# Mamba scan with a mixture of experts, one core: the load order and one pair of adds inside the scan's tile loop

## The reference

```
x = x + mamba2(layernorm(x)) + moe(layernorm(x))
```

```
Y_diag = einsum(C, B, L, xdt)          # inside a block of tokens, L the decays between two tokens
states = einsum(B, decay_states, xdt)  # what the block adds to the state
carry  = carry * chunk_decay + states  # from block to block
Y_off  = einsum(C, prev_carry, exp(dA_cs))
y = (Y_diag + Y_off + x * D) * silu(z);  y = rmsnorm(y) * norm_w;  out = y @ out_proj.T
```

## Time and profile before

| what | us |
|---|---|
| median of 3 runs | 727.1 (726.68 to 730.82) |
| the profiled execution, its own time | 727.78 |
| its span, first to last instruction | 726.0 |
| PE busy in the span | 644.9 (89%) |
| DVE busy | 509.1 (70%) |
| ACT busy | 373.9 (51%) |
| POOL busy | 316.3 (44%) |

### The profile page before, as it was taken

The page is one execution under the profiler, slowest core; times in us unless marked ns, Lnnn a source line. Parts: engine busy times, 40 slices in busy tenths (PEclk is TensorE's granted clock), DMA queues, the critical chain, the costliest instruction groups (busy, mean ns, idle before and its releaser), DMA issues.

```text
span 726.0 us, 12653 instructions
## 1 busy us (share of the span) xinstructions
PE 644.9 (89%) x4189; PEld 530.0 (73%) x4190; DVE 509.1 (70%) x1116; ACT 373.9 (51%) x787; POOL 316.3 (44%) x223
## 2 busy tenths in 40 slices
PE   4867899999999999999999999888478999999992
PEld 3757769778786777867977877564347889889981
DVE  4965976887887697788798798878866644434430
ACT  3653973754656467276375463647035644444441
POOL 1110144544452553525454425255363565665642
PEclk9968999999999999999999999999778999999996
DMA  8940112230430420403223203093277667676663
GB/s 253 332 142 29 58 61 79 97 117 30 145 118 22 154 107 12 145 32 116 99 78 117 100 18 117 1 273 105 76 207 206 113 121 141 116 132 128 116 101 43
DMA packets 32051, 80.91 MB, mean 111 GB/s; under 512 B 4801, under 2 KB 10049, under 8 KB 29825
## 3 DMA queue, kind: packets, MB, share of 16 engines
q1 hardware_dynamic: 22176, 55.22, 23.2%
q0 software_dynamic: 9056, 21.50, 16.4%
q10 hardware_dynamic: 768, 3.54, 1.6%
HBM read 60.45 MB, written 19.79 MB: 111 GB/s over the span
## 4 chain that ended last, share of the span: by engine, by line
PE 54%; DVE 13%; issue 11%; DMA 8%; ACT 6%; POOL 5%; SPq 1%; DVEq 0%; POOLq 0%; ACTq 0%
PE pi L1415 15%; PE pg L1605 11%; PE po L1454 8%; PE pd L1618 7%; DMA e<-cs_d 7%; DVE xs L917 3%; PE px L1588 2%; PE py L1492 2%; PE py L1499 2%; ACT m L647 2%; PE pxb L1572 2%; POOL y L511 1%; POOL ysq L478 1%; DVE y L1197 1%; PE phs L1628 1%
## 5 line engine op out<-in xcount | busy, mean ns | idle before, releaser
L1415 PE MATMUL pi<-xh,whl 128*128 128x256 f32 x1152 | 169.6, 291 | 5.3 <-DVE zs L923 2.8
L1415 PEld LDWEIGHTS pi<-xh,whl 128*128 128x128 f32 x1152 | 150.6, 194 | 8.6 <-issue 5.4
L917 DVE SCALAR_TENSOR_TENSOR xs<-raw,conv_w,xs 128x256 f32<-128x256 f32 x240 | 110.3, 525 | 14.3 <-ACT xs L622 14.3
L1454 PE MATMUL po<-wo,y 128*128 128x512 f32 x256 | 114.7, 601 | 2.2 <-DVE cbm L1220 1.5
L1415 PE MATMUL pi<-xl,whl 128*128 128x256 f32 x576 | 93.3, 285 | 0.0
L1454 PEld LDWEIGHTS po<-wo,y 128*128 128x128 f32 x256 | 48.1, 193 | 57.2 <-issue 55.3
L531 POOL DMA_INDIRECT out<-yo,idx x39 | 63.0, 1617 | 55.6 <-ACT yo L777 29.8
L1415 PEld LDWEIGHTS pi<-xl,whl 128*128 128x128 f32 x576 | 80.1, 192 | 0.0
L647 ACT ACTIVATE m<-m,cs_tok 128x128 f32<-128x128 f32 x256 | 79.6, 388 | 0.5
L1605 PE MATMUL pg<-ew,xgh 128*128 x312 | 66.1, 355 | 0.0
L506 POOL TENSOR_TENSOR carry<-carry,cd 128x1024 f32<-128x1024 f32 x15 | 29.0, 1934 | 84.2 <-PE py L1492 84.1
(11 more groups left out here) (203 smaller groups left out, 1180.0 us busy)
## 6 DMA issues: line engine op xcount, KB each, us to landing
m<-cs_d SPq DMA_DIRECT2D x16, 1024.0 KB, 5.6
e<-cs_d SPq DMA_DIRECT2D x32, 256.0 KB, 4.9
w_as_read<-in_w_in SPq DMA_DIRECT2D x9, 512.0 KB, 8.2
res<-in_x SPq DMA_DIRECT2D x16, 256.0 KB, 2.8
out<-o SPq DMA_DIRECT2D x16, 256.0 KB
ew<-in_w_gu SPq DMA_DIRECT2D x5, 768.0 KB, 8.9
xin<-in_x SPq DMA_DIRECT2D x6, 512.0 KB, 3.7
xn_d<-xin SPq DMA_DIRECT2D x6, 512.0 KB, 2.8
```

Of the source, the lines that this page charges most:

```text
L917: dve.scalar_tensor_tensor(out=xs[par][:, b, :], in0=raw[:, b, k:k + GT], scalar=conv_w[:, b, k:k + 1], in1=xs[par][:, b, :], op0=ALU.mult ...
L1415: mm = pe.matmul(bank[:, hf, :], whl[:, weight(g, n), lo, k, hf * P:(hf + 1) * P], xx[:, k, :], start=k3 == 0, stop=k3 == 11)
L1454: mm = pe.matmul(po[:, :], y[:, b, :], wo[:, b, :], start=b == 0, stop=b == XB - 1)
```

## The change

It does two things. In SP's loop `load_decays2(t)`, the two loads of e2 for tile t, stands ahead of `load_x(g + 2)` and of `load_decays(t + 1)`, the next tile's m; before it stood behind both. And the wait for `cdec` and `st` with the two adds to the carried state are a function `carried`, which DVE calls in even tiles ahead of `finish(t - 1)` and `own(1)`, and in odd tiles where it stood, behind `own(1)`.

```diff
                 if t == 0:
                     load_decays(1)
+                if t:
+                    load_decays2(t)
                 if c == 0 and g + 2 < G:
                     load_x(g + 2)
                 if 0 < t < T - 1:
                     load_decays(t + 1)
-                if t:
-                    load_decays2(t)
                 if c == 0 and g + 2 < G:
                     store_xn(g + 2)
...
+                def carried():
+                    dve.wait_ge(cdec, t + 1)
+                    dve.wait_ge(st, t + 1)
+                    for half in range(2):
+                        sl = carry[:, 4 * half:4 * half + 4, :, :].rearrange("p b a d -> p (b a d)")
+                        dve.tensor_tensor(sl, pxb[half][:, :, :].rearrange("p b l -> p (b l)"), sl,
+                                          ALU.add).then_inc(cadd, 1)
...
                 for n in taken[2:3]:
                     stage(g + 1, n)
+                if c == 0:
+                    carried()
                 if t:
                     finish(t - 1)
...
                 own(1)
                 if t == T - 1:
                     break
-                dve.wait_ge(cdec, t + 1)
-                dve.wait_ge(st, t + 1)
-                for half in range(2):
...
+                if c == 1:
+                    carried()
```

More of the change, by code:

```diff
@@ L1291, in vector @@
                     break
-                dve.wait_ge(cdec, t + 1)
-                dve.wait_ge(st, t + 1)
-                for half in range(2):
-                    sl = carry[:, 4 * half:4 * half + 4, :, :].rearrange("p b a d -> p (b a d)")
-                    dve.tensor_tensor(sl, pxb[half][:, :, :].rearrange("p b l -> p (b l)"), sl,
-                                      ALU.add).then_inc(cadd, 1)
+                if c == 1:
+                    carried()
                 for n in taken[3:4]:
```

## The result

The changed kernel has a median of 751.1 us over 4 runs (744.41 to 753.49), the kernel before on the same chip 726.9 (726.17 to 730.82). The ratio is 1.0307 with a 95% interval of 1.0230 to 1.0384: slower, by more than the predicted range held. The profiled execution took 749.91, its span is 748.1 against 726.0, its mean granted clock 0.955 against 0.962.

A forecast was written before the change was run, and what follows sets the result against it. PE was taken to bound the scan. The terms -2.9 + 4.0 + 0.9 + 0.5 = +2.5 us gave 730.3 for the profiled execution, and 729.6 as the predicted median, range 721.5 to 737.

The forecast's parts named there:

- the load of m in the odd tiles: m, issued behind buffer e2 in odd tiles, is 0.9 us late for DVE; hidden up to tile 11, cost nothing.
- the even tiles: Earlier load of buffer e2 returns tiles 6 and 8 to 26.75 us, load_x issued as before: -2.9 us.
- tile 13: No router there and PE already stops at off(1), so m's 0.9 us lateness goes through: +0.9 us.
- The adds' price of 4.0: Odd tiles 3 to 11: early adds push own(1), POOL's add and buffer e2, so PE waits at join: +4.0 us.
- Only PE's stops are to be had: Whole scan: it is bound by PE at a granted clock of 1.00, so only its stops can be gained.
- so the stop of 1.0 goes: Start of odd tiles: adds end at 266.6, before PE's transposes at 267.25, so PE's 1.0 us wait vanishes.
- Join's own price: PE's join L1386 in odd tiles: an idle time of 1.5 to 2 us, ended by ACT L599, replaces the adds' stop.
- +0.9 and +0.5: Later m: +0.9 us in tile 13, and +0.5 us for tile 15's m, issued behind buffer e2 in tile 14.
- The third rival: m's load bounds odd tiles at L940 if landing takes over 6.8 us; 8.5 us over tiles 3 to 11, 741.3 us; chance 0.13.
- The adds' stop at tile 15 goes as well: Tile 15: the adds' stop vanishes, but DVE then waits for ACT's btok, so the effect is 0.
- The rule on the ring: DMA queue: by in-order descriptors, removing m ahead of buffer e2 would help; the trace was read as showing no earlier landing.
- The estimate of 3.2 us for e2: Buffer e2's 512 KB load: 2.0 us plus bytes at 436 GB/s gives 3.2 us; the trace's 4.0 was used.

The follow-up runs named there:

- e5: Kernel before, loads unchanged; in even tiles DVE does own(1), then the adds, then finish(t - 1): 750.5 us, ratio 1.0270.
- e3: Kernel before with the loads of buffer e2 ahead of x and m in even tiles only, adds as before: 731.7 us, ratio 1.0020.
- e2: As a run, not the buffer: kernel before with the adds alone moved as in the change, loads as before: 738.6 us, ratio 1.0120.
- e6: The adds-only kernel with L932 of the odd tile's first stage moved behind xdt: 740.1 us, measured once.
- e4: Changed kernel, but in odd tiles m is loaded ahead of buffer e2 as before: 741.6 us, ratio 1.0197 against the kernel before.
- e9: Kernel with own(1), adds, then finish in even tiles, plus m of the tile after next issued at ydiag ahead of the store: 728.4 us, ratio 1.0001.
- e10: Kernel with adds between own(1) and finish and m issued early, plus load order x, buffer e2, m in even tiles: 726.2 us, ratio 0.9975.
- e8: Kernel before, but in odd tiles the load of m also waits for yadd, so is issued right ahead of buffer e2: 748.2 us, ratio 1.0284.

## Why the prediction was wrong

The sum was +2.5 us, and the span grew by 22.1. Three terms of it failed: the load of m in the odd tiles, put at nothing up to tile 11 (7.9 us); the even tiles, put at -2.9 (+3.4); and tile 13, put at +0.9 (+5.4). The adds' price of 4.0 held in the steady tiles and failed in tile 3. A lower granted clock was in no term at all.

*"Only PE's stops are to be had", "so the stop of 1.0 goes".* The second is right: L1520 waits for nothing. The first holds in the tiles 3 to 11 of the changed kernel, where the clock stays at 1.00. It doesn't in the tiles 12 and 13 and behind 15, where 6.4 of the 7.1 us of longer busy time lie, nor in the odd tiles of e5. The prediction had the clock at 1.00 from the profile before, and put at nothing, without a word, that longer stops could lower it.

*"So that load_x is issued at 239.6 as before": -2.9.* The issue is as late as was said, 1.1 us behind e2's (243.45, then 244.58 in tile 6). But the step took the issue for the landing. Behind e2's 512 KB, x landed in 5.0 us in the median for 3.7, in e3 in 6.4, and its reader L817 waited. The even tiles lost instead: their sum is 1.6 us shorter, but it held the five stops at L1514 of 1.0 that are gone, so the rest is 3.4 us longer, 1.5 of it PE's busy time in tile 12 at the lower clock. e3 has the same loads there and gains nothing. The kernel before shows the queueing itself. The issues of its tile 10, where x, m and e2 go out in this order within 1 us:

```profile
m<-cs_d SPq DMA_DIRECT2D x1, 1024.0 KB, 5.8
xin<-in_x SPq DMA_DIRECT2D x1, 512.0 KB, 3.5
e<-cs_d SPq DMA_DIRECT2D x2, 256.0 KB, 6.9
```

In its tiles 4, 6, 8 and 10 x, the first, took 3.5 to 4.7 us, m, the second, 5.8 to 8.5, and e2, the third, 6.9 to 8.2, against 5 and 4 for m and e2 in the odd tiles 3 to 11, where they are apart. So the late e2 is in the main its place in the queue, and putting e2 first passed the delay to x and m. Not all of it is: with the same place and the same neighbours m took 5.8 to 6.1 us in the tiles 2, 4 and 10 and 8.5 in 6 and 8, the two where PE stopped. That part stays open, as the prediction left it.

*"Two things are pushed: L964 and own(1)", and own(1) costs what stands behind it on POOL and SP: +4.0 over the tiles 3 to 11.* In the steady tiles this price is right: e2 takes 2.9 us more from tile 4 to tile 13, and the prediction's 0.8, 0.7, 0.6 and 0.7 are 2.8. In tile 3 it is 5.7 for 1.2 (8.6 for 4.0 in all), since m and e2 landed late there and the clock fell behind the stop at join (see e2). The mechanism has a hole all the same. What was followed was the chain from POOL to e2, ACT and join. Not followed was what POOL's later add does to DVE itself. It stood in the kernel before already: L932 starts at 268.87 inside POOL's L511 (267.25 to 269.62) and takes 1.30 where it takes 0.68 elsewhere. Its two inputs and its output are in SBUF; it ends 0.55 us after POOL does, whatever its own start. With L511 1.2 us later, L932 ends, xdt starts and the router starts 1.2 later. e2 showed the stop, e6 took the cause away and the stop with it, but not the time: join took it over. The Trainium skill (SBUF — State Buffer, "Who interferes with whom") says that a DVE instruction with two SBUF inputs and a GpSimd instruction reading SBUF contend for one pair of ports, and the second is fully blocked; the trace agrees, with 2.50 us against 0.68. The 1.2 us went through the router wait (1.35 for 1.0), and a smaller rest at join (0.2 to 0.5; 2.6 in tile 3) added to it. Join's own price was right: 1.8 in tile 5 once nothing stood ahead of it (e6). That the sum over the steady tiles came out right is partly luck, as PE stood at the router and not at join.

*"It lands at 277.25", with the 5.3 of tile 7: "Cost: nothing, unless m takes more than 6.8 us", +0.9 and +0.5.* This is the largest hole. m took 7.0 to 8.7 us in the odd tiles. e4 differs from the changed kernel by this order alone, and its tiles 3, 5, 7, 9 and 11 take 160.8 us for 168.7. The third rival had this mechanism, its point, 6.8 us, and nearly its price, 8.5 for these tiles, and gave it 0.13. The 5.3 had been read from a tile where m had 2.55 us of the queue to itself; the text said so of e2 and didn't apply it to m. In tile 13 off(1) waits 5.00 us for 2.61, of which the adds alone make 3.31 (e2), and PE is 1.65 longer busy there, at 0.95: so +0.9 was 5.4. That the whole is above this rival's 741.3 too has the even tiles and the clock as its known parts; that its 2.4 us of slack were drawn on by the later router and POOL's later work as well is argued, not shown.

*"The orders on PE, ACT and POOL are the same"* hid one more thing: the store, the load of res and m stand behind `finish(t - 1)` on SP's queue. The change pushes finish by 1.2 us. e5 pushed it by more and showed what that queue can cost: m came up to e2, and e2 paid 2.3 us.

*"The adds' stop at tile 15 goes as well, but DVE then waits for btok: 0".* Right: 2.17 at L1514 became 2.48 at L1527, which waits for btok.

*The rule on the ring.* The prediction put the megabyte ahead of e2 at nothing, since m was issued 2.55 us earlier, and used that trace against the Trainium skill (DMA: Bandwidth & Descriptors, "Queues, rings and completion order"), by which a ring's descriptors are taken in order. Both hold: with m 2.55 us ahead ACT had e2 4.85 us after its issue, with m 0.44 ahead after 7.15 (e5). The Trainium skill's rule spoke against this change, for the transfers that would now stand second, and it was weighed only for the one that came first. The estimate of 3.2 us for e2, from "Anatomy of one DMA" in the Trainium skill, rests on a formula given there for loads that GpSimd issues. These are issued by SP, and took 3.7 to 4.8 us with nothing close ahead of them.

What stays open: why e9 and e10, with half of the adds' stops gone, aren't faster. In their profiled executions PE stood still 5.0 and 7.5 us less than in that of the kernel before (76.1 and 73.6 for 81.1), but was busy 7.0 and 4.2 us more, at clocks of 0.90 to 0.94 in the tiles 8, 12 and 13. Over all their runs the medians of the mean clock, 0.957 and 0.959, are those of the kernel before (0.958), so this may belong to the profiled executions alone, and doesn't settle it. The clock does go with the spread of one kernel's runs: of the 59 runs of the kernel before that took under 735 us, the ten fastest (to 725.5) had a mean clock of 0.958 to 0.969, the ten slowest (from 731.2) 0.952 to 0.960. It isn't shown when a stop is followed by the lower clock: 1.82 us at off(1) of tile 12 was in e2, and 1.81 was not in the kernel before. Nor is it shown why m took 5.8 us in tile 10 and 8.5 in tile 6, nor what makes L883 slow in the tiles 3 and 7 of the changed kernel alone.

## What to carry to other kernels

A stop of the busy engine can have two prices, the wait itself and a lower granted clock behind it: compare the busy time for the same work, not the idle time alone. When an operation is moved ahead, list what it pushes, and for each pushed operation everything that waits for it: on other engines, in the in-order queue of the DMAs, and every operation of another engine that it would then run beside. An operation whose time differs between two places of the same trace (1.30 and 0.68) is a sign of such sharing and should be explained before anything near it is moved; whether it costs anything only a run without it tells. A landing time belongs to the transfer's place in the queue: take it from a row with the same neighbours at the same distance, and spend a slack only once over all edits that draw on it.

## What the runs showed of the hardware

- DVE's L932 (both inputs in SBUF) took 0.68 us, and 1.30 or 2.51 by how much of POOL's add was left, ending 0.55 us after it both times. xdt, with one input in PSUM, took 1.28 beside the same add. A product of 32 columns (L883, 0.18 us normally) took 1.88 beside POOL's L506, and L940, of 16 columns, 1.90 for 0.17 beside POOL's L495 (e2). It goes the other way too: L495 took 3.98 for 1.93 beside DVE's product with the mask.
- Two transfers issued within about 1.5 us on one queue: the first landed as if alone, the second some 2 us or more later: m 7.4 for 5.3 (changed kernel, tile 7), e2 5.7 to 6.2 for 3.9 to 4.6 (e8), x 6.2 to 7.0 for 3.5 to 4.7 (e3). With 2.55 us between m and e2 neither was late in the tiles 3 to 11; in tile 13 of the kernel before they took 7.0 and 5.7 at the same distance, for a reason that isn't shown.
- PE's busy time for the same matmuls of an odd tile was 30.1 us at a granted clock of 1.00 and 33.2 at a mean of 0.90 (tile 7 of e9 and e5). In e5 the fall came behind a stop of 2.44 us at join: the next 10 us had a mean of 0.69.
